# Wide attention: the query and key projections moved ahead of the transposes and the output product on TensorE

## The reference

```python
def cross_attention(x, ctx, wq, wk, wv, wo, bo):      # ctx = x for self attention
    q, k, v = heads(x @ wq), heads(ctx @ wk), heads(ctx @ wv)
    attn = jax.nn.softmax(einsum('bhnd,bhmd->bhnm', q, k) * SCALE, axis=-1)
    out = einsum('bhnm,bhmd->bhnd', attn, v)
    return merge(out) @ wo + bo
...
x = cross_attention(layer_norm(x, g1, be1), layer_norm(x, g1, be1), wq1, wk1, wv1, wo1, bo1) + x
x = cross_attention(layer_norm(x, g2, be2), context, wq2, wk2, wv2, wo2, bo2) + x
return geglu_ff(layer_norm(x, g3, be3), w_ff1, b_ff1, w_ff2, b_ff2) + x
```

## Time and profile before

| | |
|---|---|
| median of 3 runs | 3690.57 us (3687.29 to 3707.21) |
| profiled execution, its own time | 3695.35 us |
| its span in the profile | 3693.5 us |
| busy over the span | PE 98%, PEld 84%, DVE 63%, ACT 57%, POOL 34% |
| self stage, first to last scores group (tile view) | 1184.0 to 2330.3 us |
| cross stage, first to last scores group | 2365.4 to 3424.6 us |
| mean of the copies outT (L1319), both stages | 0.69 us |
| transfers in both stages | next to none (DMA share 0.00 to 0.01) |

### The profile page before, as it was taken

How to read it: one execution, slowest core, us unless ns; L and a number is a source line. 1 busy time by engine, 2 the same in 40 slices (tenths; PEclk the granted TensorE clock), 3 DMA queues, 4 the chain that set the end, 5 groups by cost and what they waited for, 6 DMA issues and landing times. The chain is left out here.

```text
span 3693.5 us, 98205 instructions
## 1 busy us (share of the span) xinstructions
PE 3606.9 (98%) x37983; PEld 3119.7 (84%) x37983; DVE 2315.9 (63%) x3922; ACT 2095.1 (57%) x5165; POOL 1252.6 (34%) x1273
## 2 busy tenths in 40 slices
PE   7999999999998999999999999899999999999999
PEld 5777778778887888898889888788888888888888
DVE  5788866664554666666666667555555555556554
ACT  3777777774445555555555555455555555555343
POOL 3333333332442333333333333333223222323342
PEclk7999999999999999999999999999999999999999
DMA  3444333232001000000000000000000000000000
GB/s 77 112 110 116 95 82 93 79 85 73 2 0 35 2 1 0 0 0 0 0 0 0 0 0 1 26 4 1 2 2 2 1 2 2 2 1 1 20 19 24
DMA packets 99546, 98.72 MB, mean 27 GB/s; under 512 B 31248, under 2 KB 74128, under 8 KB 99344
## 3 DMA queue, kind: packets, MB, share of 16 engines
q1 hardware_dynamic: 93408, 94.41, 9.9%
q0 software_dynamic: 5120, 1.35, 0.2%
q10 hardware_dynamic: 816, 0.08, 0.0%
HBM read 20.76 MB, written 5.24 MB: 7 GB/s over the span
## 5 line engine op out<-in xcount | busy, mean ns | idle before, releaser
L1213 POOL TENSOR_TENSOR a_probs<-a_probs,a_rsums 128x1024 f32<-128x1024 f32 x160 | 303.7, 1898 | 754.1 <-DVE a_rsums L1338 754.1
L1251 ACT ACTIVATE a_probs<-a_scores_banks,a_negmax 128x128 f32<-128x128 f32 x1280 | 367.4, 377 | 285.3 <-DVE a_negmax L1326 282.7
L1213 POOL TENSOR_TENSOR c_probs<-c_probs,c_rsums 128x616 f32<-128x616 f32 x160 | 204.6, 1279 | 757.4 <-DVE c_rsums L1338 757.3
L711 ACT ACTIVATE s_probs<-s_scoresT_banks 128x1024 f32<-128x1024 f32 (+1 forms) x320 | 327.4, 1023 | 193.1 <-PE s_scoresT_banks L895 190.8
L1251 ACT ACTIVATE c_probs<-c_scores_banks,c_negmax 128x77 f32<-128x77 f32 x1280 | 313.1, 335 | 197.4 <-DVE c_negmax L1326 197.2
L797 DVE TENSOR_REDUCE s_negmax<-s_scores_banks 128x8 f32<-128x1024 f32 (+1 forms) x320 | 322.3, 1007 | 147.7 <-PE s_scores_banks L877 143.3
L1319 DVE COPY c_outT<-c_out_bank 128x512 f32<-128x512 f32 x160 | 110.7, 692 | 367.6 <-PE c_out_bank L1498 307.2
L1319 DVE COPY a_outT<-a_out_bank 128x512 f32<-128x512 f32 x160 | 110.6, 692 | 293.9 <-PE a_out_bank L1498 240.7
L1667 DVE SCALAR_TENSOR_TENSOR f_hidden<-f_value_bank,bias,f_gate 128x512 f32<-128x512 f32 x160 | 120.1, 751 | 247.1 <-ACT f_gate L1642 245.2
L676 POOL DMA_DIRECT2D s_q_stack<-s_shift x160 | 93.6, 585 | 494.6 <-ACT s_shift L734 488.7
L1326 DVE TENSOR_REDUCE a_negmax<-a_scores_banks 128x4 f32<-128x512 f32 x320 | 206.1, 686 | 87.5 <-PE a_scores_banks L1397 87.5
(11 more groups left out here) (315 smaller groups left out, 10612.3 us busy)
## 6 DMA issues: line engine op xcount, KB each, us to landing
s_q_stack<-front SPq DMA_DIRECT2D x192, 160.0 KB, 3.3
s_k_stack<-front SPq DMA_DIRECT2D x96, 160.0 KB, 3.8
s_out<-s_heads SPq DMA_DIRECT2D x128, 80.0 KB, 2.4
s_k_stack<-front SPq DMA_DIRECT2D x96, 96.2 KB, 2.9
x_tokens<-in_x SPq DMA_DIRECT2D x16, 320.0 KB, 3.4
out_x<-x_tokens SPq DMA_DIRECT2D x16, 320.0 KB, 2.4
s_q_stack<-s_shift POOLq DMA_DIRECT2D x160, 8.0 KB, 2.6
s_ctx_in<-in_ctx SPq DMA_DIRECT2D x16, 115.5 KB
```

What stands on the lines that cost most here:

```text
L711: nc.scalar.activation(probs[i][0:NK, :, :], scoresT[0:NK, :, :], ACT.Exp).then_inc(s_exp, 1)
L1213: nc.gpsimd.tensor_tensor(probs[i][:], probs[i][:], rsums[(k - 1) % 2][:].unsqueeze(2).broadcast_to([P, UNIT, NK]), ALU.mult).then_inc(s_p ...
L1251: done = nc.scalar.activation(probs[i][:, h, :], scores[:, h // GROUP, h % GROUP * NK:(h % GROUP + 1) * NK], ACT.Exp, bias=negmax[k % 2][: ...
```

## The change

In both wide stages (the function is shared) TensorE's step puts the two projections of query and key tiles right behind the scores (and the transposes at places 3 and 4), and the transposes of the probabilities and the output product behind them. The values projection and the heads' output stay where they are. ACT copies tile 0 out behind four exponentials, where it was six. DVE's `ctx_low` goes from the end of its step at place 4 to the head of that step, ahead of `outT`. No instruction is added or taken away.

```diff
@@ ACT step
-                exponentials(q, k, 0, 6)
+                exponentials(q, k, 0, 4)
                 tile_out(q, k, 0)
-                exponentials(q, k, 6, 8)
+                exponentials(q, k, 4, 8)
                 tile_out(q, k, 1)
                 values_out(q, k)
@@ DVE step
                 if s == 1 and which:
                     which.wait_stats(dve, ahead)
+                context_n = context_at(q, k)
+                if s == 4 and context_n is not None:
+                    par = (k // GROUPS) % 2
+                    dve.wait_ge(crossing.s_high, context_n + 1)
+                    nc.vector.tensor_tensor(ctx_low[par][0:CTX_D, :], odd_bank[0:CTX_D, 0:PAIR * NKC],
+                                            ctx_high[par][0:CTX_D, :].bitcast(F32), ALU.subtract).then_inc(s_ctx_split, 1)
                 if live(n - Y_LAG, WUNITS):
                     dve.wait_ge(s_out, n - Y_LAG + 1)
...
-                context_n = context_at(q, k)
-                if s == 4 and context_n is not None:
-                    par = (k // GROUPS) % 2
-                    dve.wait_ge(crossing.s_high, context_n + 1)
-                    nc.vector.tensor_tensor(ctx_low[par][0:CTX_D, :], odd_bank[0:CTX_D, 0:PAIR * NKC],
-                                            ctx_high[par][0:CTX_D, :].bitcast(F32), ALU.subtract).then_inc(s_ctx_split, 1)
                 if s == 4 and which:
                     which.vector_split(dve, ahead, (k // GROUPS) % 2)
@@ TensorE step
+                project(q, k, 0)
+                project(q, k, 1)
                 transpose_step(q, k - T_LAG)
                 output_step(q, k - Y_LAG)
-                project(q, k, 0)
-                project(q, k, 1)
                 project_values(q, k)
                 values_step(q, k - T_LAG)
```

## The result

The changed kernel takes 3710.61 us (median of 20 runs), the kernel before 3692.3 us (median of 20). The ratio is 1.0053, 95% interval [1.0034, 1.0071]: a slowdown of 0.5%, and no change (1.0) lies outside the interval. One of the 20 runs before and two of the 20 after were some 4% longer at a lower clock; the ratio leaves them out. The profiled execution has a span of 3708.8 us against 3693.5, 15.3 us more. The forecast was +10.7 us and 3701 us.

The account below looks back on a forecast made before the run. PE's order of work was taken to bound both wide stages. Self +5.9 us and cross +4.8 us gave +10.7 us, 3706 on the profiled 3695.35; with the runs' median 4.8 us lower, 3701 us (+0.3%), range 3685 to 3718 us.

Parts of the forecast that it names:

- The place of the time: Both wide stages: the order of PE's work decides; other engines count only where PE waits for them.
- Place 3, the new wait: Tile 1 waits for ACT's `pair_y` to leave `odd_bank`: net +0.14 us in the self stage, +0.38 us in cross.
- Place 4 of the cross stage: Tile 1's wait for `ctx_low` shrinks to 0.20 us in place of 0.47: -0.27 us.
- The thin cover for the heads' output: Cross stage, place 4: `probsT` ends near 2829.45, the heads' output is due near 2829.7; covered by 0.2 us.
- Rival B: Cross stage, place 4: DVE late, heads' output waits 0.2 + 0.08 us, 30 times; +8 us, 3710 us; chance 0.10.
- the reading of the DVE page: Drain rule read strictly: DVE's successors start 0.1 us later each, heads' output waits about 0.2 us, 6 us in all.
- Plain steps, the new neighbours: Three changed boundaries between PE's groups: +0.01 us a step, range 0 to +0.06, +0.05 us a pair.
- the prediction's own sign: Prediction wrong if a plain step changes by 0.03 us or more, or ACT or DVE is later than covers allow.
- the third boundary: Output product to values projection: same kinds on both sides as the boundary it replaces, so no cost.
- Rival A: fp32 behind fp32r, or projection behind scores, costs 0.05 us more in each of 320 steps; 27 us, 3717 us; chance 0.14.
- the old waits: Kernel before: 0.33 us a self pair, 0.20 + 0.47 us a cross pair; 30 us, 0.8% of the time.
- the main case's own range: Main case, 3701 us, chance 0.66: 3693 to 3709 us from the base and rounding of waits.

Follow-up runs that it names:

- e_place3: The changed kernel with TensorE's old order (transposes, output product, then projections) at place 3 alone; ratio 0.9949 against the kernel before, span 3668.1 us.
- e_both: The kernel before with only ACT's and DVE's edits of the change, TensorE's order left old; ratio 0.9982 against the kernel before, span 3679.7 us.
- f_matmul_t: The kernel before with the eight transposes of probabilities done as plain fp32 matmuls against the identity; ratio 1.0700, span 3933.8 us.
- e_yfirst: The kernel before with the output product ahead of the transposes, right behind the scores; ratio 1.0147, span 3754.2 us.
- e_tfirst: The changed kernel with the transposes of probabilities kept right behind the scores, projections next; ratio 0.9927 against the kernel before, span 3658.5 us.
- f_best: The kernel before with ACT's and DVE's edits of the change, and the output product behind the projections at place 4 only; ratio 0.9920, span 3663.7 us.

## Why the prediction was right, and where it was off

**The place of the time.** PE bounds both stages, and what counts are its starts. That held inside the pairs: every difference in their steps is in a wait or a switch on PE. The first and last pairs and the passage between the stages changed too, and the sum had no term for them (see the balance).

**Place 3, the new wait.** Forecast +0.14 us in the self stage and +0.38 in the cross stage, measured 8.01 - 7.87 = 0.14 and 7.48 - 7.13 = 0.35. That `pair_y` is the cause is shown by the start of tile 1, 0.05 us behind its end, and by e_place3, which takes the wait away and gains 32 us.

**Place 4 of the cross stage.** Forecast -0.27 us, measured 6.77 - 7.03 = -0.26. The thin cover for the heads' output held: 2842.86 - 2842.57 = 0.29 us, forecast 0.2. Rival B and the reading of the DVE page do not occur in this kernel. That the DVE edit alone costs 0.27 us at this place (e_both against before) was not seen in the prediction, and didn't have to be for the sum.

**Plain steps, the new neighbours.** This is the term that was mis-sized. The prediction took +0.01 us a step; the four self steps without a new wait grew by 0.04 to 0.05 and the three plain cross steps by 0.03 to 0.06. By the prediction's own sign (wrong if a plain step changes by 0.03 us or more) this term failed, and the time came out within the stated range because the others held and this one is small. A self pair grew by 0.31 us in place of 0.19, 31 x 0.12 = 3.7 us more than forecast, and a cross pair by 0.20 in place of 0.16. The growth of the plain steps lies at one boundary only, scores to projection. Between projection and transposes nothing was lost: eight transposes take 1715.58 - 1714.70 = 0.88 us there. Between output product and projection the third boundary is as before: the first interval behind the output product is long there too, with no switch (kernel before, 1703.08 - 1702.85 = 0.23 us), but the eight output matmuls give way after 1702.85 - 1701.87 = 0.98 us, where eight at their pace of 0.136 would take 1.09, so nothing is lost. Rival A had named the boundary that did cost (a projection behind the scores), but with 0.05 us more in each of 320 steps, 16 us; the runs show about 0.03 more than the forecast in some 210 of them.

The mistake was in the choice of the nearest row. The switch from tiled to full matmuls shows as one longer interval behind it, and I took it from a projection in the first stage, whose stationary side has 80 columns and whose load takes 0.15 us by its timeline, against 0.19 us for the 128 columns here. The trace of the kernel before held a nearer row, a group with 128 columns behind the same tiled group of the first stage, and a short one that warns against a rule by the load alone:

```profile
139.60 0.34 PE L325 MATMUL s_odd_bank<-s_w_high,quad_high 128*128 128x160 f32 x1
139.78 0.28 PE L325 MATMUL s_odd_bank<-s_w_low,quad_high 128*128 128x160 f32 x1
139.89 0.28 PE L325 MATMUL s_odd_bank<-s_w_high,quad_low 128*128 128x160 f32 x1
...
858.58 1.19 PE L963 MATMUL s_even_bank<-s_k_stack,s_w_high 128*128 128x512 f32 x4
859.61 0.60 PE L1001 MATMUL s_max_bank<-s_sums,select 80*80 80x128 f32 x4
```

The four matmuls of 512 columns take 859.61 - 858.58 = 1.03 us, where four at their pace of 0.23 take 0.93: 0.10 us for the switch, as it then came out. What the runs show:

| group behind the scores | its weight load | first interval over the others |
|---|---|---|
| transposes (before, self stage) | 0.14 us | 0.93 - 0.88 = 0.05 us |
| projection (after) | 0.19 us | 0.22 - 0.12 = 0.10 us |
| transposes (before, cross stage) | 0.15 us | 0.935 - 0.873 = 0.06 us |
| plain matmuls against the identity (f_matmul_t, cross stage) | 0.15 us | 1.81 - 1.75 = 0.06 us |
| output product (e_yfirst) | 0.19 us | 1.19 - 1.09 = 0.10 us |
| plain matmuls against the identity (f_matmul_t, self stage) | 0.19 us | 1.89 - 1.78 = 0.11 us |

In these rows neither the type of the data nor the kind of matmul matters, the duration of the first load does: what shows is that duration less 0.08 to 0.09 us. The page TensorEngine Tiling (Array Packing) of the Trainium skill, section Tiling Modes, says that changing the mode drains TensorE; these rows agree that the switch costs time and add that the next load is then in the open. That the loads can't be started ahead over the switch is my reading of the rows; no run shows it directly. The rows at 139.60 set a limit to the table: there the load is 0.19 us and the first interval 0.18, the second 0.11, only 0.07 more. So the load alone does not set the cost of every group. These are shorter fp32r matmuls (160 columns) than the projection's; why less shows there was not tested. The same was seen in small in e_tfirst, without a switch: behind a matmul of 154 columns a load of 0.19 us shows by 0.04 us.

**The balance.** In the pairs of the changed kernel ACT's and DVE's edits, with an order of TensorE that suits them, remove the old waits: 30 us, as the prediction said of the kernel before. TensorE's new order takes back 32 us at place 3 (e_place3), 31 x 4 x 0.04 + 30 x 3 x 0.04 = 9 us of exposed loads at the other places, and 30 x (6.77 - 6.63) = 4 us at place 4 of the cross stage, where tile 1 still waits for `ctx_low`. That sums to -30 + 45 = +15 us, and the measured figure from the first self scores on is 15.0. That the two agree so well is luck in part. By the steps the pairs grew by 31 x 0.30 + 30 x 0.20 = 15 us (means over the middle pairs), but the stages from first to last scores group only by 7.5 + 5.6 = 13.1 us: the first and last pairs, which have other steps, gave 2 us back. The passage between the stages, at a lower clock, then added 2.5. The forecast of 3701 us was 9.6 us below the median of 3710.6, which lies just above the main case's own range (3693 to 3709 us) and inside the wider one. Of that, 4.6 us are the sum's; 1.7 us are the base (20 runs before have a median of 3692.3, the three that I had 3690.6); the rest, some 3 us, is that the profiled executions differ by less than the medians do (15.3 against 18.3 us). Kept behind the transposes, the projections pay little of it: e_tfirst and f_best are 30 and 34 us faster than the kernel before over the same stretch.

## What to carry to other kernels

When matmul groups are reordered on a TensorE that is never idle, price each boundary by the weight load of the group that follows it, and take the price from a row with the same number of stationary columns: behind a switch of tile size put the group with the shortest loads. And when a group moves ahead, look at what the groups in between had covered: 1.96 us of transposes and output product had hidden ACT's reading of a bank, and the transposes alone (0.87 us) would have been enough (e_tfirst). A move on a second engine (DVE's `ctx_low`) can be right in one order of TensorE and wrong in another, so try them together and apart.

## What was not expected of the hardware

- A transpose on TensorE has a weight load of 0.14 us, where a plain matmul with the same 128 x 128 stationary side has one of 0.19 us. With 77 columns, in the cross stage, both take 0.15 us. As a plain fp32 matmul against the identity, each of the eight becomes two in the profile, and the plain steps grow by 0.97 us in the self stage and 0.87 in the cross stage.
- Parts of the program that no edit touches differ between executions: the first self scores group starts anywhere from 1174.6 to 1188.1 us. Differences below some 10 us in the whole span had to be read from the stage itself.
